# Mixture-of-experts rows put in expert order while attention runs: scatters in place of gathers, in a decoder layer on one core

## The reference

```python
x = _layernorm(x + _L0_attn_ref(x, ...))           # 16 heads of 64, causal
x = _layernorm(x + _L0_xattn_ref(x, ctx_1024, ...)) # 16 heads of 16, masked
# ffn, for each of two groups of experts:
logits = x2 @ router_w; scores = softmax(logits)
expert_weights, expert_indices = lax.top_k(scores, 2)
order = argsort(flat_e); xs = x2[tok]              # rows sorted by expert
ys = ragged_dot(silu(ragged_dot(xs, wg)) * ragged_dot(xs, wu), wd) * flat_w
out_g = zeros_like(x2).at[tok].add(ys)
x = _layernorm(x + (out0 * 2 + out1 * 2) / 4)
```

## Time and profile before

| what | us |
|---|---|
| median of 3 runs | 5787.31 |
| the profiled execution, its own time | 5787.89 |
| its span, first to last instruction | 5786.2 |
| stage 1 (to the start of stage 2) | 0 to 4156 |
| stage 2, tiles without combining | 4193 to 4770 |
| stage 2, tiles with combining | 4770 to 5441 |
| stage 3 | 5441 to 5786 |
| PE busy, POOL busy, DVE busy | 5104.9, 2811.6, 4065.0 |

### The profile page before, as it was taken

How to read it: one execution, slowest core, us unless ns; L and a number is a source line. 1 busy time by engine, 2 the same in 40 slices (tenths; PEclk the granted TensorE clock), 3 DMA queues, 4 the chain that set the end, 5 groups by cost and what they waited for, 6 DMA issues and landing times. The chain is left out here.

```text
span 5786.2 us, 125535 instructions
## 1 busy us (share of the span) xinstructions
PE 5104.9 (88%) x35657; PEld 4132.5 (71%) x35657; DVE 4065.0 (70%) x19675; ACT 3418.5 (59%) x13128; POOL 2811.6 (49%) x2856
## 2 busy tenths in 40 slices
PE   7999999999999999999999999999489997777400
PEld 6888888888888888888888888887367875555300
DVE  4778777877787787778777777877564434444477
ACT  4777777777777777777767777777334443333222
POOL 3344443444444443444444443444345547777676
PEclk9999999999999999999999999999799999999755
DMA  2000000000000000000000000000255567777666
GB/s 85 21 20 19 22 19 21 19 23 20 19 22 19 20 19 23 18 21 21 20 20 19 22 19 21 18 23 16 81 182 156 157 181 205 207 207 206 190 204 192
DMA packets 355913, 404.42 MB, mean 70 GB/s; under 512 B 63283, under 2 KB 309046, under 8 KB 354742
## 3 DMA queue, kind: packets, MB, share of 16 engines
q1 hardware_dynamic: 263782, 229.82, 12.4%
q0 software_dynamic: 68864, 143.50, 9.7%
q10 hardware_dynamic: 22608, 23.08, 1.2%
HBM read 265.88 MB, written 130.29 MB: 68 GB/s over the span
## 5 line engine op out<-in xcount | busy, mean ns | idle before, releaser
L522 POOL DMA_INDIRECT list_d<-token,place x512 | 510.6, 997 | 1249.8 <-DVE place L846 1132.1
L685 ACT ACTIVATE prob<-prob,negmax 128x128 f32<-128x128 f32 x2048 | 798.9, 396 | 20.7 <-DVE negmax L753 19.2
L685 ACT ACTIVATE xprob<-xprob,xnegmax 128x128 f32<-128x128 f32 x2048 | 794.0, 393 | 2.4 <-DVE xnegmax L753 2.3
L703 ACT COPY probT<-bank 128x512 f32<-128x512 f32 x512 | 300.9, 588 | 782.0 <-PE bank L634 781.9
L1098 POOL DMA_INDIRECT xg<-x_d,who x576 | 546.2, 948 | 380.4 <-DVE who L1279 300.4
L490 POOL TENSOR_TENSOR yTl<-yT,yTh 128x256 fp32r<-128x256 f32 x512 | 405.7, 793 | 577.7 <-DVE yTh L898 575.1
L1167 PE MATMUL bank<-moe,xgT 128*128 x2304 | 615.9, 391 | 12.9 <-DMA moe<-g 12.9
L1291 DVE COPY y<-bank 128x256 f32<-128x256 f32 x576 | 244.4, 424 | 486.1 <-PE bank L1183 463.0
L616 PE MATMUL bank<-kD,qT 128*128 128x256 f32 x2048 | 578.7, 405 | 0.0
L626 PE MATMUL bank<-xkD,xqT 128*128 128x512 f32 x1024 | 523.7, 593 | 0.6 <-DVE xnegmax L753 0.6
L753 DVE CUSTOM_DVE_ANT_0 prob<-bank,causal 128x128 f32<-128x128 f32 x2048 | 471.8, 286 | 44.9 <-PE bank L616 42.1
(11 more groups left out here) (227 smaller groups left out, 14960.3 us busy)
## 6 DMA issues: line engine op xcount, KB each, us to landing
y_d<-y SPq DMA_DIRECT2D x576, 128.0 KB
xT_s<-xT SPq DMA_DIRECT2D x128, 128.0 KB, 2.6
x<-x SPq DMA_DIRECT2D x128, 128.0 KB, 2.0
cT<-cT SPq DMA_DIRECT2D x128, 128.0 KB, 2.0
x_d<-x SPq DMA_DIRECT2D x128, 128.0 KB, 2.0
x2c<-x_d SPq DMA_DIRECT2D x128, 128.0 KB
acc_d<-acc SPq DMA_DIRECT2D x128, 128.0 KB
sum<-acc_d SPq DMA_DIRECT2D x128, 128.0 KB, 3.1
```

Of the source, the lines that this page charges most:

```text
L522: nc.gpsimd.indirect_dma_start(list_d[:, :], bass.IndirectOffsetOnAxis(ap=place[p][:, j:j + 1].bitcast(U32), axis=0), token[p][:, :], None ...
L685: last = nc.scalar.activation(dst[:, h, :], dst[:, h, :], ACT.Exp, bias=src_bias[:, h:h + 1], scale=-1.0, accum_out=acc[:, h:h + 1])
L703: nc.scalar.copy(probT[:, :, :].rearrange("p h q -> p (h q)"), T[:, :]).then_inc(probT_in, 1)
```

## The change

**Stage 1.** POOL scatters the rows of x2 themselves, as two halves of 512 bytes, to `xs_d[group][half]` at row `expert * 16384 + rank`, and a code (token * 4 + choice, 4 bytes) to `list_d[group]` at the same row: 12 indirect DMAs a batch instead of 4, of the batch one iteration later (lag 5), four in each of the sub-steps 0, 2 and 3. x2 and `place` have three buffers instead of two; DVE's write of x2 also waits for the scatters of the batch three before (`placed`). There is one iteration more at the end. The clearing at the start is 4 DMAs of 2 MB (rows of 512 bytes) and 2 of 16 KB.

**Stage 2.** A tile is loaded by SP as two blocks of 64 KB and its codes as one row, from a row number in a register; 10 buffers. Each fourth tile PE turns four rows of codes, and DVE takes the larger of code and a spare row's number (`to`). POOL scatters a tile's y by `to` to `y_d`, where each token has 4 rows of 1 KB side by side. So the combining of group 0 needs no gather: ACT loads 2 KB a token (and x2), DVE adds, SP stores. Gone are the lists' gather and transposes, `who`, `want`, `look_up`. The weights' first load is ACT's; the others are SP's, one of five pieces every third tile, from tiles 12, 40 and 304 on.

**Stage 3.** SP loads a quad's rows as one DMA of 1 MB and `acc_d` as one of 0.5 MB, 4 deep; POOL does the root by a power and two small operations; ACT stores a quad in one DMA.

```diff
                 def iteration(t):                                   # POOL, stage 1
-                            if s == 3:
-                                place_tokens(t)
...
+                            if t.live(5):
+                                scatter(t.item(5), s)
+                    def scatter(b, s):
+                        p = b % 3
+                        if s == 0:
+                            if b == 0:
+                                pool.wait_ge(list_clear, 16 * CLEARS)
+                            pool.wait_ge(place_ready, b + 1)
+                            pool.wait_ge(x2_ready, b + 1)
+                        for j in range(SLOTS):
+                            where = bass.IndirectOffsetOnAxis(ap=place[p][:, j:j + 1].bitcast(U32), axis=0)
+                            if s == 0:
+                                nc.gpsimd.indirect_dma_start(list_d[j // TOPK][:, :], where, code[:, b, j:j + 1], None).then_inc(placed[p], 16)
+                            elif s >= 2:
+                                k = s - 2
+                                nc.gpsimd.indirect_dma_start(xs_d[j // TOPK][k][:, :], where, x2[b % 3][:, k * P:(k + 1) * P], None).then_inc(placed[p], 16)
...
+                    for g in range(NGRP):                           # SP, start of stage 1
+                        sp.dma_start(list_d[g].rearrange("(e n) o -> e (n o)", n=N)[:, 0:P], nobody[:, :]).then_inc(list_clear, 16)
+                        for k in range(KC):
+                            sp.dma_start(xs_d[g][k].rearrange("(e n) d -> n e d", n=N)[0:P, :, :], blank[:, :, :].broadcast_to([P, E, P])).then_inc(list_clear, 16)
...
+                            q = n % NX                              # SP, stage 2, every tile
+                            sp.reg_load(rows[q], firsts[0:1, n:n + 1])
+                            wait(sp, xgt_made, n - NX + 1)
+                            row = sp.snap(rows[q], min_val=0, max_val=E * N - P)
+                            for k in range(KC):
+                                sp.dma_start(xg_s[q][:, k * P:(k + 1) * P], xs_d[g[0]][k][bass.ds(row, P), :]).then_inc(xg_in[q], 16)
+                            l = t.u % NL
+                            if t.p == 0:
+                                wait(sp, coded, t.u - NL + 1)
+                            sp.dma_start(codes[l][t.p:t.p + 1, :], codes_of[g[0]][:, bass.ds(row, P)]).then_inc(codes_in[l], 16)
                         if b and b.live(2):
                             p = b.slot(2)
                             sp.wait_ge(acc0_ready, b.item(2) + 1)
...
+                            nc.gpsimd.indirect_dma_start(           # POOL, stage 2, every tile
+                                y_d[:, :], bass.IndirectOffsetOnAxis(ap=to[t.turn(3) % 2][:, q:q + 1].bitcast(U32), axis=0),
+                                y_s[q][:, :], None).then_inc(y_out[q], 16)
...
+                            wait(act, part_ready, b.item(2) + 1)    # ACT, stage 2, combining
+                            act.dma_start(x2c[p][:, :], x2_d[bass.ds(b.item(0) * P, P), :]).then_inc(x2c_in[p], 16)
+                            wait(act, acc0_ready, b.item(2) + 1)
+                            act.dma_start(rows0[p][:, :, :].rearrange("p j d -> p (j d)"),
+                                          y_of_token[b.item(0) * P:(b.item(0) + 1) * P, 0:TOPK * D]).then_inc(rows0_in[p], 16)
...
+                        wait(sp, rows_used, (n - DEPTH + 1) * QUAD) # SP, stage 3, every quad
+                        sp.dma_start(rows1[h][:, :, :], of_quad(y_of_token[:, TOPK * D:SLOTS * D], n)).then_inc(rows_in[h], 16)
+                        sp.dma_start(sum0[h][:, :, :], of_quad(acc_d, n)).then_inc(sum0_in[h], 16)
```

More of the change, by code:

```diff
@@ L203, in decoder_layer @@
[L203 to L231, removed]
+        def load_experts(eng, dst, first, gate, up, down, done, piece):
+            if piece < 2 * KC:
+                k, j = divmod(piece, 2)
+                eng.dma_start(dst[:, :, piece * HID:(piece + 1) * HID],
+                              (gate, up)[j][first:first + HALF, k * P:(k + 1) * P, :].rearrange("e p h -> p e h")).then_inc(done, 16)
+            else:
+                eng.dma_start(dst[:, :, KC * 2 * HID:WCOL],
+                              down[first:first + HALF, :, :].rearrange("e p d -> p e d")).then_inc(done, 16)
@@ L337, in pipeline @@
             def pipeline(eng, iteration):
-                for i in range(-4, NB + 4):
+                for i in range(-4, NB + 5):
                     iteration(at(i, 4, 0, NB))
@@ L984, in decoder_layer @@
             tabs = sb("tabs", [1, P * TA // PACK], I32)
+            spans, firsts = sb("spans", [P, 3, TA], I32), sb("firsts", [1, P * TA], I32)
+            low, high = sb("low", [P, NT], I32), sb("high", [P, NT], I32)
+            beside = [sb(f"beside{i}", [P, NT]) for i in range(3)]
+            row_no = sb("row_no", [P, 1])
+            spare_no = sb("spare_no", [P, SPARE])
+            spare = sb("spare", [P, NT])
             PLACES = 3 * HALF
@@ L1016, in decoder_layer @@
             y_out = [sem(f"y_out{q}") for q in range(NQ)]
-            want0_ready, part_ready, acc0_ready = sem("want0_ready"), sem("part_ready"), sem("acc0_ready")
+            part_ready, acc0_ready = sem("part_ready"), sem("acc0_ready")
             rows0_in, x2c_in, acc0_out = ([sem(f"{n}{p}") for p in (0, 1)] for n in ("rows0_in", "x2c_in", "acc0_out"))
             GROUP_U = TILES // NQ
+            LOADED = 16 * KC
+            LAST_LOAD = TILES + 16
+            NEXT_LOAD = {tile + 3 * piece: (n, piece) for n, tile in ((1, 12), (2, 40), (3, LAST_LOAD)) for piece in range(PIECES)}
             FIRST_U = GROUP_U + 5
@@ L1291, in iteration @@
                             v.tensor_copy(y_s[q][:, :], YB[q % 2][:, 0:D]).then_inc(y_in, 1)
+                        if t.live(0) and t.p == NQ - 1:
+                            dve.wait_ge(coded, t.u + 1)
+                            for q in range(NQ):
+                                wait(dve, y_out[q], (t.u - 1) * 16)
+                            v.tensor_tensor(to[t.u % 2][:, :], CB[:, 0:NQ], spare[:, t.u * NQ:(t.u + 1) * NQ], ALU.max).then_inc(to_ready, 1)
                         if t.live(1):
@@ L1362, in _ @@
                 def _(sp):
-                    def body(n, h, u):
-                        for q in range(QUAD):
-                            wait(sp, rows_used, (n - 2) * QUAD + (q + 1))
-                            sp.dma_start(sum0[h, q][:, :], acc_d[bass.ds((n * QUAD + q) * P, P), :]).then_inc(sum0_in[h, q], 16)
-                    quads(sp, body)
+                    for n in range(QUADS):
+                        h = n % DEPTH
+                        wait(sp, rows_used, (n - DEPTH + 1) * QUAD)
+                        sp.dma_start(rows1[h][:, :, :], of_quad(y_of_token[:, TOPK * D:SLOTS * D], n)).then_inc(rows_in[h], 16)
+                        sp.dma_start(sum0[h][:, :, :], of_quad(acc_d, n)).then_inc(sum0_in[h], 16)
@@ L1398, in _ @@
+                    for h in (0, 1):
+                        act.wait_ge(out_done[h], 16 * (QUADS // 2))
                 @block.vector
```

420 lines of the change are left out of this document (171 added, 249 removed).

## The result

| | us |
|---|---|
| before, median of 7 runs | 5787.07 (5784.47 to 5789.66) |
| changed, median of 7 runs | 5847.37 (5822.06 to 5867.13) |
| ratio, 95% interval | 1.0107 (1.0085 to 1.0129) |
| changed, profiled execution and its span | 5864.81, 5862.8 |

What follows compares the result with a forecast made beforehand. PE was taken to bound attention and the tiles before the combining, POOL's gathers the combining and stage 3. Terms 8 - 15 + 27 - 30 - 99 + 5 - 126 = -230 against 5787.89 gave 5558 us, 4.0% less; range 5430 to 5720.

Steps and rivals of the forecast that it cites:

- Start, +8: Start: clears grow by 4.2 MB, 14 us at 303 GB/s, part fitting before the first x; +8 us (0 to +12).
- Stage 1, -15: Attention: twelve scatters a batch fit POOL's idle time and never wait for `place`; -15 us (-24 to +10).
- the 83 of the prediction: Stage 1: DVE's cross-attention product at 0.69 instead of 1.98 us, all of that on 64 iterations; 83 us.
- Rival three: Stage 1: scatters of 512-byte rows hold POOL longer than 4-byte ones; at 2.5 us each about 6540 us; chance 0.06.
- End of stage 1, +27: After attention's last work: 48 scatters left, 60.5 us, and 3 more to land; +27 us (+10 to +35).
- Stage 2 up to the combining, -30: Tiles before the combining: SP the near limit at 1.5 to 1.75 us, 1.73 taken; -30 us (-50 to +20).
- Rival two: Stage 2: a DMA with its row in a register costs more to issue; +181 us, 5739 us; chance 0.14.
- With the combining, -99: Stage 2 with the combining: SP late next, 2.15 us a tile for 2.52 over 269 tiles; -99 us.
- The chain over `acc0_ready`: Stage 2 with the combining: `acc_d` store waits for DVE's sums, loads behind it; 8.1 to 9.3 us around four tiles.
- Stage 3, -121: Stage 3: DMAs at 340 GB/s, 220 us for 346, -126; with +5 for the last scatter's landing, -121.
- Rival four: Stage 3: stays a matter of DMA at today's 196 to 205 GB/s, 327 us; 5665 us in all; chance 0.08.
- Rival one: Stage 2 with the combining: SP's issues cost less than counted, DMAs pace at 1.8 us a tile; 5465 us; chance 0.12.

Runs made afterwards that it cites:

- e3: Changed kernel with the start's clears walking each expert's rows in order, blank rows read from 32 partitions: 6056.89 us (1 run), kernel before 6062.31 beside it.
- e9: Changed kernel with codes' loads issued by ACT, acc_d store a pair later, clears behind the first loads of x: 5834.64 us, 0.9482 of the kernel before.
- e7: Changed kernel with whole 1 KB rows of x2, acc_d store a pair later, clears behind the first loads of x: 5500.08 us, 0.9062 of the kernel before.
- e4: Changed kernel with x2's rows kept whole (1 KB; one scatter and load for two; 8192 rows an expert): 5691.43 us, 0.9380 of the kernel before.
- e1: Changed kernel in effect unaltered, the added register load being absent from the program that ran: 6091.15 us (1 run), kernel before 6062.31 beside it.
- e5: Changed kernel unaltered, on another chip: 6102.73 us, 1.0060 of the kernel before.
- e6: Changed kernel with whole 1 KB rows of x2 and the acc_d store a pair later with four acc0 buffers: 5516.21 us, 0.9090 of the kernel before.
- e11: Changed kernel with whole rows and later acc_d store, plus four scatters of 4-byte codes a batch (twelve): 5749.25 us, 0.9476 of the kernel before.
- e12: Changed kernel with whole rows and later acc_d store again (eight scatters a batch), beside e11: 5518.60 us, 0.9109 of the kernel before.
- e10: The kernel before, unaltered, profiled on another chip: 6162.81 us (1 run), median of the kernel before 6158.48 beside it.
- e2: Changed kernel with the acc_d store one pair of tiles later and four acc0 buffers for two: 5980.19 us, 0.9851 of the kernel before.
- e8: Changed kernel with a second register load and one register operation more a tile on SP: 6328.59 us (1 run), kernel before 6067.91 beside it.

## Why the prediction was wrong, step by step

**Start, +8 against +42.** The step took the rate of the clears before, 303 GB/s in DMAs of 256 KB, for pieces of 512 bytes that lie 8 MB apart, which run at 139. And it let DMAs be issued and forgotten, where SP stands in an issue for 12.8 to 17.2 us with x's loads behind it. e3's other order takes 17 us off. e9, with the same pieces behind the first loads of x, has its first scores at 50.3 and e7 at 51.8, against 52.5 of before: with the clears at another place in SP's list the whole delay is gone.

**Stage 1, -15 against -17.** Right on the first chip in what was to be seen: twelve scatters of 0.97 to 1.02 us fit in POOL's idle time, none waits for `place`, and DVE's cross-attention product takes 0.72 us on average instead of 0.89 (none of the 512 is over 1.2 us, where 62 were). That is 87 us less of DVE, near the 83 of the prediction. The size was luck in part: the -15 was chosen below the 83, not worked out. Rival three is out: a scatter of 512-byte rows takes 1.02 us, one of 1 KB rows 1.10 (e4). The rule that POOL and VectorE share the way to SBUF (the Trainium skill, "GPSIMD Engine Reference", Key points), weighed in the prediction, did not decide: DVE's two-input products became shorter. But the term holds for the first chip alone. On three other chips twelve scatters cost 1.4 to 1.7 us a batch over eight (e1 and e4, e5 and e6, e11 and e12), and on that of e9 and e10 twelve cost 1.6 us over the four of before, some 200 us in 128 batches, which no term had.

```profile
L497 POOL DMA_INDIRECT xs_d<-x,place x1024 | 1047.6, 1023 | 277.7 <-issue 277.7
L494 POOL DMA_INDIRECT list_d<-code,place x512 | 498.2, 973 | 138.3 <-issue 137.9
...
L743 DVE TENSOR_TENSOR xprob<-xprob,xinv 128x512 f32<-128x512 f32 x512 | 367.5, 718 | 17.7
```

The last in the kernel before:

```profile
L770 DVE TENSOR_TENSOR xprob<-xprob,xinv 128x512 f32<-128x512 f32 x512 | 454.2, 887 | 17.6
```

**End of stage 1, +27 against +29.** Right: 48 scatters are left at 4136.3 and the last ends at 4200.3. With e4's eight a batch in place of twelve this stretch is 29 us shorter than e1's.

**Stage 2 up to the combining, -30 against +101.** This is the step that failed, at "SP becomes the near limit: 1.5 to 1.75". Its list was right and its sizes were not. The register load was taken from PE's row, 0.30; SP's takes 0.49. Register work and gaps were "0.1 to 0.3" and are 0.4. The parts as written come to 1.48 to 1.86, not to 1.75 at most, so that even their own upper end lay above PE's 1.71. The rare long issues (1 to 2.4 us) were seen for weights alone. 2.0 and their share make 2.14, and above PE's 1.71 every 0.1 us of SP is 31 us. I put the value at PE's pace though the register load's nearest row was another engine's and the register work had no row at all. Rival two, an issue by register that costs more, had 2.1 and 2.4 us a tile and 5739 us: the nearest in mechanism, with a chance of 0.14. The first tile's 27.4 us (28 forecast) was right.

**With the combining, -99 against +77.** The chain over `acc0_ready` was named and was there, and e4 shows it at 9.5 us for four tiles in the stretch shown, 10.3 on average, where 8.1 to 9.3 was written. What failed is the step from two costs to one: the text set chain (2.0 to 2.3) and SP's list (1.95) side by side and took the larger. They lie in one queue: SP's issuing of two tiles is itself a part of the chain, and while SP stands at the wait its list isn't worked off. So 2.15 us a tile was forecast and 2.84 measured. e2 takes the wait away (2.74 to 2.34 us a tile), e4 shortens the list (to 2.57), and both together give 1.90.

**Stage 3, -121 against -155.** Right in kind, 34 us too careful: 2 KB rows and DMAs of 1 MB are moved at 354 GB/s, where 340 was taken, and filling and draining, put at 22 us, cost about 5. Rival four, today's rate of 196 to 205 GB/s, is out.

**Rival one** (issue time small beside the transfer, by the Trainium skill's page "DMA: Bandwidth & Descriptors", Issuing engines are not separate DMA queues) was given 0.12 and is wrong here: three issues of 0.28 to 0.39 us and one register load a tile were the bound, at a DMA share of 0.43. e9 moves one of the issues to ACT, with the bytes unchanged, and a tile before the combining takes 1.83 us where the changed kernel takes 2.20.

## What to carry to other kernels

Count what one tile costs the queue that issues its DMAs as one counts an engine's instructions: on SP here 0.49 us for a register load, 0.33 to 0.39 for a load of 128 rows, 0.28 for one row, some 0.07 for every register instruction between. Apart from that sum, a wait for results in the same list turns prefetch off (e4, with a list of 1.85 us a tile by e6's expectation, ran at 2.57; e6, with the store later, at 1.90): put the store of a result at least one step later, with more buffers. Another engine for the store was not tried here. Large clears go behind the first loads, not ahead of them.

## What the hardware showed beyond this

- SP stood in one DMA's issue for 12.8 to 17.2 us at the start, while clears of 2 MB issued before it were still being written.
- Of two register loads in a row on SP the first took 0.49 us and the second 0.28 (e8).
- Writes of 512 bytes from SBUF to rows 8 MB apart ran at 139 GB/s in 16 to 90 us; walked in order, and read from 32 partitions, the window from 16 to 70 us had 191 GB/s and first scores came 17 us earlier.
- The changed kernel's own runs spread by 0.8% (5822 to 5867) where those of before spread by 0.1%; e7's by 0.1% (5495 to 5501).
- The same kernel before takes 5787, 6061 to 6068, or 6158 us, by chip.
